# The order in which a pair's sums, the next pair's maxima and the block sums are turned, taken and queued in a fused attention and feed-forward kernel

## The reference

```python
def _L0_attn_ref(x, ...):                     # x: (4, 2048, 256), 16 heads of 16
    xn = _ln(x, ln1_g, ln1_b)
    q, k, v = split_heads(xn @ w_in.T + b_in)
    scores = einsum('bhqd,bhkd->bhqk', q, k) / sqrt(16)
    allowed = (idx % 8 == 0)[:, None] | (idx[:, None] == idx[None, :])
    attn = softmax(where(allowed, scores, -inf))
    x = x + einsum('bhqk,bhkd->bhqd', attn, v) @ w_out.T + b_out
    h = gelu(_ln(x, ln2_g, ln2_b) @ w1.T + b1)          # 1024 wide
    return x + h @ w2.T + b2

x = _layernorm(x + _L0_attn_ref(x))
# feed-forward: base = x @ wi.T, the expert of the row (argmax of 8 gates) adds a rank-4 term,
# relu, then @ wo.T
x = _layernorm(x + _L0_ffn_ref(x))
```

## Time and profile before

| | |
|---|---|
| median of 3 runs | 1442.03 us (1438.64 to 1444.67) |
| the profiled execution | 1439.25 us, of which the span from first to last instruction is 1437.5 us |
| TensorE (PE) busy | 1364.4 us, 95% of the span |
| VectorE (DVE) busy | 852.9 us, 59% |
| ScalarE (ACT) busy | 732.3 us, 51% |
| GpSimd (POOL) busy | 647.6 us, 45% |
| attention stages | about 160 to 310, 483 to 653, 825 to 995, 1166 to 1316 us |

### The profile page before, as it was taken

How to read it: one execution, slowest core, us unless ns; L and a number is a source line. 1 busy time by engine, 2 the same in 40 slices (tenths; PEclk the granted TensorE clock), 3 DMA queues, 4 the chain that set the end, 5 groups by cost and what they waited for, 6 DMA issues and landing times.

```text
span 1437.5 us, 26427 instructions
## 1 busy us (share of the span) xinstructions
PE 1364.4 (95%) x10103; PEld 1073.2 (75%) x10103; DVE 852.9 (59%) x1823; ACT 732.3 (51%) x1103; POOL 647.6 (45%) x533
## 2 busy tenths in 40 slices
PE   6799999999999999999999999999999999999997
PEld 5688665578888766668888866667888866557886
DVE  6747566746656576655647566753665656663332
ACT  3444555553444555654444466555344455556442
POOL 3554321337764323246865422334776432132755
PEclk9899999999999999999999999999999999999999
DMA  7565123216662132212672213311566212310100
GB/s 243 162 177 108 39 50 78 56 34 194 192 146 71 35 76 51 57 44 90 204 214 69 66 34 80 71 40 35 192 190 148 72 42 42 77 26 30 52 16 30
DMA packets 91393, 130.49 MB, mean 91 GB/s; under 512 B 8314, under 2 KB 68180, under 8 KB 88148
## 3 DMA queue, kind: packets, MB, share of 16 engines
q1 hardware_dynamic: 91268, 128.82, 32.9%
HBM read 68.08 MB, written 60.57 MB: 90 GB/s over the span
## 4 chain that ended last, share of the span: by engine, by line
PE 78%; DVE 8%; POOL 5%; issue 4%; ACT 2%; DMA 0%; SPq 0%; POOLq 0%; DVEq 0%; ACTq 0%
PE ps L1659 19%; PE ps L1660 16%; PE ps L1661 16%; PE ps L1848 8%; PE ps L1837 7%; PE ps L1822 4%; PE ps L1895 2%; PE ps L1917 2%; PE ps L1883 2%; POOL rows L1122 2%; DVE stats L1404 2%; DVE mx L1530 1%; DVE x1in L1425 1%; DVE xn L1492 1%; ACT prob L1260 1%
## 5 line engine op out<-in xcount | busy, mean ns | idle before, releaser
L1530 DVE TENSOR_REDUCE mx<-ps 128x2 f32<-128x1024 f32 x256 | 311.1, 1223 | 177.4 <-PE ps L1822 174.4
L1260 ACT ACTIVATE prob<-ps 128x1024 f32<-128x1024 f32 x256 | 262.1, 1024 | 156.9 <-PE ps L1837 156.1
L1137 POOL TENSOR_TENSOR hid1l<-gel,hid1h 128x512 fp32r<-128x512 f32 x85 | 111.2, 1308 | 207.3 <-ACT hid1h L1302 207.0
L1137 POOL TENSOR_TENSOR hid0l<-gel,hid0h 128x512 fp32r<-128x512 f32 x86 | 112.2, 1305 | 184.9 <-ACT hid0h L1302 184.8
L1137 POOL TENSOR_TENSOR hid2l<-gel,hid2h 128x512 fp32r<-128x512 f32 x85 | 110.8, 1304 | 168.6 <-ACT hid2h L1302 168.5
L1294 ACT ACTIVATE gel<-ps,cols 128x512 f32<-128x512 f32 x128 | 88.1, 688 | 181.2 <-PE ps L1661 170.0
L1296 ACT ACTIVATE gel<-ps 128x512 f32<-128x512 f32 x128 | 76.5, 598 | 140.4 <-PE ps L1917 139.9
L1837 PEld LDWEIGHTS ps<-qslot,kslot 50*128 50x128 f32 x1024 | 76.4, 185 | 82.2 <-issue 46.0
L1837 PE MATMUL ps<-qslot,kslot 50*128 50x256 f32 x1024 | 129.4, 331 | 4.0 <-ACT prob L1260 3.6
L1848 PE MATMUL ps<-prob,vals 128*32 128x256 f32 x2048 | 124.6, 382 | 0.0
L1822 PE MATMUL ps<-kslot,qslot 48*128 48x512 f32 x512 | 102.7, 411 | 7.9 <-DVE mx L1530 7.5
(11 more groups left out here) (246 smaller groups left out, 3972.2 us busy)
## 6 DMA issues: line engine op xcount, KB each, us to landing
k_d<-kst SPq DMA_DIRECT2D x192, 128.0 KB
kslot<-k_d SPq DMA_DIRECT2D x64, 384.0 KB
xin<-in_L_attn_x SPq DMA_DIRECT2D x32, 256.0 KB, 4.4
rows<-xs_d SPq DMA_DIRECT2D x16, 512.0 KB, 6.1
y_d<-rows SPq DMA_DIRECT2D x15, 512.0 KB, 3.1
rows<-y_d SPq DMA_DIRECT2D x15, 512.0 KB, 4.5
out<-rows SPq DMA_DIRECT2D x15, 512.0 KB, 3.2
xs_d<-xin SPq DMA_DIRECT2D x28, 256.0 KB, 3.1
```

The costliest lines, as they stand in the source:

```text
L1137: nc.gpsimd.tensor_tensor(hid[i % RING][1][:], gel[i % 2][:], hid[i % RING][0][:], ALU.subtract).then_inc(lo_done, 1)
L1260: nc.scalar.activation(prob[prob_of(*a[1:])][:].rearrange("p e i q -> p (e i q)"), ps[:, 0:2, :].rearrange("p a n -> p (a n)"), ACT.Exp).t ...
L1530: nc.vector.tensor_reduce(best[:, :, j % NQ], ps[:, at:at + 2, :], AX.X, ALU.max).then_inc(maxr_done, 1)
```

## The change

Four things are altered in the list of steps, and one wait is added.

1. The turn of a pair's sums (`ot`) is no longer asked for at `kk == 1` of the next pair but at `kk == 4`, in one entry with the turn of the maxima (`mt`) of the pair after: first `ot`, then `mt`, in the same bank, the maxima in columns of their own (from `QW` on). TensorE does not wait between the two; ScalarE's copy of `osum` waits for both turns.
2. An entry of `alone` is put where the third part of an item has no other turn of its own (`hook`), else after the first `dn` of the second half. Beside two blocks the hooks (`tn`, `tn`, `ga`, `pi`) move from items 0, 2, 4, 7 to 1, 3, 5, 7.
3. A block's `sum` goes to the front of the queue of small jobs.
4. In `visit`, `maxima` comes before `scores`.

```diff
         def turns(s):
             p, kk = s // KK, s % KK
-            if p and kk == 1:
-                alone.append([("ot", b, p - 1)])
-            if kk == 4 and p + 1 < PAIRS:
-                alone.insert(0, [("mt", b, p + 1), ("mtd", b, p + 1)])
+            if kk == 4:
+                alone.append([("ot", b, p - 1)] * (p > 0) + [("mt", b, p + 1), ("mtd", b, p + 1)] * (p + 1 < PAIRS))
...
             taken = [s]
+            maxima(s)
             scores(s)
-            maxima(s)
             if s % GROUP == GROUP - 1 or s == STEPS_B - 2:
...
-                job(0.7, ("sum", blk, h))
+                jobs.insert(h, (0.7, unit[0], (("sum", blk, h),)))
...
-        places = [(0, 2, 4, 7)] * 2 if len(blocks) == 2 else [(0, 2, 3, 7), (0, 1, 3, 7), (1, 2, 4, 7)]
+        places = [(1, 3, 5, 7)] * 2 if len(blocks) == 2 else [(0, 2, 3, 7), (0, 1, 3, 7), (1, 2, 4, 7)]
...
                 if not hook:
-                    taken = turned_out(s, False)
+                    turned_out()
             if part == parts - 1:
                 put(("ev", i))
-                turned_out(s, taken)
                 one = pending.pop(0)
                 down_part(one, 1, 0)
+                turned_out()
...
-                    nc.scalar.activation(mT[:], ps[0:2 * UNITS, BANK[(what, *a)], 0:P], ACT.Copy).then_inc(mt_done, 1)
+                    nc.scalar.activation(mT[:], ps[0:2 * UNITS, BANK[(what, *a)], QW:QW + P], ACT.Copy).then_inc(mt_done, 1)
...
                     act.wait_ge(oturn_done, n)
+                    if a in WITH_OT:
+
+                        act.wait_ge(mturn_done, N("mt", *WITH_OT[a]))
```

More of the change, by code:

```diff
@@ L293, in turns, with turned_out @@
             p, kk = s // KK, s % KK
-            if p and kk == 1:
-                alone.append([("ot", b, p - 1)])
-            if kk == 4 and p + 1 < PAIRS:
-                alone.insert(0, [("mt", b, p + 1), ("mtd", b, p + 1)])
[L299 to L303, removed]
+            if kk == 4:
+                alone.append([("ot", b, p - 1)] * (p > 0) + [("mt", b, p + 1), ("mtd", b, p + 1)] * (p + 1 < PAIRS))
+        def turned_out():
+            if alone:
+                flush("os")
                 for one in alone.pop(0):
@@ L307, in turned_out @@
                         job(1.3, ("os", *one[1:]))
-                return True
-            return taken
         def moves(s):
@@ L337, in visit @@
                     weighted(one)
+                maxima(s + 1)
                 scores(s + 1)
-                maxima(s + 1)
                 taken.append(s + 1)
@@ L401, in attention @@
                 down_part(one, 0, 1)
-                taken = bool(hook)
                 if hook and hook[0][0] == "pi":
                     flush("pick")
-                    if alone and alone[0][0][0] == "mt":
-                        turned_out(s, False)
                 for step in hook:
@@ L559, in bank_of @@
     return OUT
-BANK, EARLIER = {}, {}
+BANK, EARLIER, WITH_OT = {}, {}, {}
 _latest = {}
@@ L597 @@
         for _n in _banks:
-            if _n in _latest and _latest[_n] not in EARLIER[_s]:
+            if _w == "mt" and _latest[_n][0] == "ot":
+                WITH_OT[_latest[_n][1:]] = _s[1:]
+            elif _n in _latest and _latest[_n] not in EARLIER[_s]:
                 EARLIER[_s].append(_latest[_n])
@@ L1826, in step @@
                     pe.wait_ge(negs_done, 2 * N("ng", *a))
-                    nc.tensor.transpose(ps[0:2 * UNITS, bank, 0:P], negs[:].rearrange("p e h t -> p (e h t)"), ident[:]
+                    nc.tensor.transpose(ps[0:2 * UNITS, bank, QW:QW + P], negs[:].rearrange("p e h t -> p (e h t)"), ident[:]
                                         ).then_inc(mturn_done, 1)
```

## The result

| | before | with the change |
|---|---|---|
| median | 1438.69 us (1438.50 to 1444.67, 5 runs) | 1405.10 us (1404.26 to 1406.32, 5 runs) |
| ratio | | 0.9755 [0.9734, 0.9775] |
| the profiled execution | 1439.25 us | 1405.79 us, span 1404.0 us |

The kernel became 2.45% faster. The forecast was 1414 us with a range of 1404 to 1428: the direction is right, the time lies at the low end of the range, and about a quarter of the gain (9 of 34 us) was not foreseen.

A forecast was written before the change was run, and what follows sets the result against it. TensorE was taken to set the time, with most lost beside two blocks. Removed 35.0 less added 5.1, 3.1 and 1.0 gave 25.8 us off: 1413.5 from the profiled 1439.25, 1416 from the median; forecast 1414, range 1404 to 1428.

The forecast's parts named there:

- splits: Beside two blocks, the maxima's turn no longer waits for VectorE's split of a block's turned rows: 13.3 us removed.
- gates: The maxima's turn no longer waits behind the gates in the attention stages: 4 x 0.65 = 2.6 us removed.
- turns: The sums' turn no longer waits behind the maxima's turn in their bank: 10 x 0.60 = 6.0 us removed.
- copy: Beside two blocks, VectorE's copy of the sums no longer holds up a reduction: eight stalls of 1.1, 8.8 us removed.
- The split of turned rows ahead of a reduction: Beside two blocks, VectorE's split delays the next reduction and so the next maxima: 8 x 0.64 = 5.1 us added.
- Maxima first: Beside two blocks, VectorE's chain of 1.84 us exceeds the 1.80 between maxima by 0.04, some 78 times: 3.1 us added.
- Small VectorE work: `os` always falls into a short interval, taking about 0.8 us where it has 0.6: 1 us added.
- The gate inputs: At one place in batches 1 and 2 the sums wait for the copy of `pi`, instead of `pi` for `mT`: 0.
- The first: Nothing takes the place of the removed stalls, the added terms being near nothing: 1404 us, chance 0.10.
- The second: VectorE becomes the bound beside two blocks, its small jobs and splits delaying the maxima: 1426 to 1432 us, chance 0.12.
- The third: Scores behind maxima start without weights loaded, in about 204 visits: 20 us (1434) or 41 us (1454), chance 0.08.
- The fourth: ScalarE's copies of sums and maxima delay `mtd`, so the next pair's scores wait for the DMA: 1440 us, chance 0.02.

The follow-up runs named there:

- experiment 10: The changed kernel with the block sum put back at the end of the queue of small jobs: 1407.23 us, ratio 0.9766.
- experiment 4: The kernel before with only the hooks beside two blocks moved from items 0, 2, 4, 7 to 1, 3, 5, 7: 1414.66 us, ratio 0.9835.
- 5: The changed kernel with the hooks beside two blocks back on items 0, 2, 4, 7: 1410.28 us, ratio 0.9787.
- 7: The changed kernel with maxima taken over 256 of every 512 columns only, so each reduction is shorter: 1396.72 us, ratio 0.9694.
- experiment 1: The kernel before with only the maxima's products put ahead of the scores' in each visit: 1439.92 us, ratio 1.0008.
- 2: The changed kernel with the scores' products put ahead of the maxima's again: 1402.21 us, ratio 0.9758.
- experiment 3: The kernel before with only a block's sum moved to the front of the queue of small jobs: 1444.98 us, ratio 1.0046.
- 9: The kernel before with only the sums' and maxima's turns joined in one entry at kk == 4, with one wait for both: 1419.21 us, ratio 0.9848.

## Why the prediction was right on the direction and short on the size

**How the terms are measured.** A stage beside two blocks is a chain of 51 intervals, each from the start of one maxima step to the start of the next. Each interval is compared with the shortest one that holds the same steps in the same order, in any of the kernels with that order of a visit. What it is longer by was lost.

**Removed, 35.0 us: right.** My terms for a stage beside two blocks were 6.65 (splits), 1.3 (gates), 0.6 (turns) and 4.4 (copy), 12.95. In before the intervals that hold these stalls are longer by the same: 4.05 us with `tn` and `mt` against 2.36 with `tn` alone (1.66, and 0.03 for the turn itself), 2.82 with `mt` and `ot` against 2.25, and 3.23 with the first `ot` of a pair's sums against 1.92 with no turn (1.1, and 0.22 for the turn itself). Beside three blocks the terms were 2.4 and 2.15, 4.55; the stages gained 4.46 and 4.41. Experiments with edits alone bear them out: the splits, gates and `mT` are out of the list of waits; the block sums were 4.3 and are 3.75 (experiment 10). What I did not see is that the terms beside two blocks are not independent. Hooks alone brought 9.6 us in batch 0 and the joined turns alone 6.9, together 11.4, not 16.5. As the whole change was forecast, this did no harm to the sum. The expectations for its parts missed for the reason of the next paragraph, the price of what is added: 18.9 us by the stages where 15 was expected in experiment 4 (3.6 of it charged for splits and small work, which with scores first cost 0.11 to 0.13 a split), and 7.0 where 9.2 was expected in 5.

**Added, 9.2 us: the failed step.** The intervals of the changed kernel lose 5.9 us beside two blocks (3.05 in batch 0, 2.8 in batch 3), and beside three about nothing. Two of the three terms were too large, the third too small.

- *The split of turned rows ahead of a reduction*, 8 x 0.64: the mechanism is there, 8 times, at 0.35 (2.8 us). I took the maxima 0.80 behind the turn (it is 0.88), the split's end 1.96 after it (the reduction's record starts at 1.87), and no slack in the interval; but this interval holds the second half of `dn` and an `up`, and takes 1.90 to 1.94, not the 1.80 of the earlier trace rows, against a chain of 1.84. The three are 0.08, 0.09 and 0.06 to 0.10, and bring my 0.61 down to 0.34 to 0.38. I had taken one interval of three for all.
- *Maxima first*, 78 x 0.04 = 3.1: the intervals that were 1.80 are 1.82 or 1.83 where nothing else falls in. These are 18 in the two stages, not 78: 0.6 us. In the longer intervals, three of four, the chain of 1.84 has room.
- *Small VectorE work*, 1.0: four intervals in each stage, three with `os` and one with `pick`, are 2.01 to 2.14 instead of 1.78, at 0.22 to 0.36 each: 2.0 us, twice the term.
- The rest, some 0.5 us, are steps of 0.03 that before has too.
- *The gate inputs*, 0: `ot` waits behind `pi` for 0.58 us once in each stage beside three blocks, in place of `pi` behind `mT` (0.60). Right.

**Put at nothing.** Before loses 1.7 and 1.5 us a stage beside two blocks (the fall of the clock aside) in small waits of up to 0.4 us that are none of the named stalls. My sum kept them, as if the added waits came on top; but the added 5.9 is all that the changed kernel loses, so that these 3.2 are to be taken off it. So a stage gains 12.95 + 1.7 - 3.05 = 11.6, measured 11.4, and 12.95 + 1.5 - 2.8 = 11.65, measured 11.5. By the stage lengths what was added on balance is 3.3 us, not 9.2.

**The clock, not in the sum.** Before's profiled execution lost 1.57 us in batch 3 to a fall of the granted clock that the changed kernel's does not have. With it the account closes: 25.8 forecast, 5.9 added too much on balance (9.2 less 3.3), 1.6 clock, 33.3. Against the median of before the clock counts for more, some 3 us (last section).

**The range.** Its bounds were not added up rightly: upward the two terms leave 8.2 and 4.7 us, 12.9 together, where the text has 8.2 and reaches 1424. The measured time lies at the other end, where both are near nothing.

**The rivals.** The first (nothing takes the place of the stalls, 1404) was nearer than my own case, and half right: something took their place, but a third of what I gave. The second (VectorE the bound) was wrong beside two blocks: VectorE's chain costs some 5.9 us there, of which short reductions take out 4.3 (7). The third fell with the trace and with experiments 1 and 2. The fourth did not show: beside two blocks `mT` has been copied 0.8 us after the maxima's turn started (224.82 to 225.61), and no scores wait for its DMA.

## What to carry to other kernels

When work moves behind the bottleneck engine's step, price the new stall in the very interval into which it falls, with that interval's own length, and not with the shortest one on the page. Stalls that share a bank or a queue are not a sum: test the edits alone and together before pricing them singly, since here the plainest one, four numbers in a table, held 18.9 of the 31.7 us. And where two orders of a visit tie by the whole time, compare them by stage: each was better in one kind of stage.

## What the hardware showed that was not expected

**VectorE held by GpSimd.** In experiment 3 two tiny multiplications (two SBUF inputs each) started while a GpSimd `tensor_tensor` ran and ended with it, 2.12 and 1.30 us for 0.19. Before has it too: at 307.10 one takes 1.33 us and ends 0.05 behind the GpSimd pass of 307.08 to 308.38. The Trainium skill, page "SBUF — State Buffer", section "SBUF: two separate sides", says that a VectorE operation with two SBUF inputs blocks wholly when a GpSimd operation that reads SBUF has started first. By that rule each should end with the GpSimd pass; the trace agrees within 0.04 us for these two. It does not agree for another kind of pass: at 283.03 in before the same two multiplications take 0.19 and 0.18 us while GpSimd's `tensor_scalar` on the rows, which reads SBUF as well, runs from 282.50 to 283.80.

```profile
281.30 2.50 POOL L1122 TENSOR_SCALAR rows<-rows,mv,rstd 128x256 f32<-128x256 f32 x2
...
283.03 0.29 DVE L1570 TENSOR_TENSOR otok<-osum,rsum 128x32 f32<-128x32 f32 x2
```

The reductions and splits, which read PSUM, do not show the hold: at 252.77 in the changed kernel a reduction takes its 1.22 us beside a GpSimd pass.

**TensorE's clock.** The granted clock of the attention stages is 1.00 (2.4 GHz) in most executions, but in some it falls to half (1.2 GHz) for some us. Windows of the kernel before, batch 3:

```profile
1196.00:1198.00 2.00, 1.37 (x11) 0.97 (x12) 0.60 (x2) 0.90 (x3) 2.00 (x2) 1.00 0.02 4
1198.00:1200.00 2.00, 2.00 (x8) 1.25 (x10) 1.66 (x6) 0.76 (x1) 1.14 (x2) 0.57 0.03 6
1200.00:1202.00 2.00, 2.00 (x9) 1.43 (x10) 0.98 (x1) 1.02 (x1) 0.79 (x1) 0.57 0.00 0
```

And of experiment 1, batch 0:

```profile
248.00:250.00 2.00, 0.59 (x7) 0.35 (x5) 0.87 (x2) 1.33 (x3) 0.28 (x1) 1.00 0.02 4
250.00:252.00 2.00, 2.00 (x15) 1.57 (x15) 1.00 (x1) 1.03 (x2) 1.01 (x1) 0.93 0.00 1
252.00:254.00 2.00, 2.00 (x9) 1.07 (x7) 0.49 (x2) 0.27 (x1) 0.00 (x0) 0.50 0.00 1
254.00:256.00 2.00, 2.00 (x10) 1.36 (x10) 0.96 (x1) 1.26 (x2) 0.00 (x0) 0.71 0.00 0
```

Both times TensorE had stood for the split of a block's rows shortly before (1.41 us idle at `mt`, as in the earlier trace rows); another fall of experiment 1, at 292 us, follows the maxima's turn behind the gates. Experiment 1 has four such falls inside its attention stages, the kernel before one, experiment 3 three, one of them while TensorE stood the 4.4 us. The other nine kernels have none there, also not the two that still stand behind a block's rows (5 and 9). What decides whether a fall follows is open: seven of the eight long waits of before are followed by none, and one profiled execution of each kernel is too few.

What the falls are worth in the medians can be read from the granted clock of each run. The 40 runs of before beside the experiments took 1434.38 to 1447.97 us, at clocks of 0.994 down to 0.984. The seven of them at 0.994 took 1434.38 to 1436.35, median 1435.57; those at 0.990, eleven in all, 1437.59 to 1442.86. The changed kernel's five runs had 0.993 or 0.994 and took 1404.26 to 1406.32. So at like clock the change is worth 30.5 us, 2.1%, and some 3 of the median's 33.6 us are the clock. Whether the change brings these 3 us too, by taking the long stalls away, is not shown: the nine kernels with shorter stalls or none had no fall in the one execution of each that was profiled.
